# Channel attention and retention of a four-layer decoder rewritten as one pipeline of eight groups

## The chip, the core and the metric

The kernel runs on one core of one Trainium2 chip. The metric is the device time of one execution in microseconds (us), lower is better. Engines are named as the profile names them: PE (TensorE matmuls), PEld (TensorE weight loads), DVE (VectorE), ACT (ScalarE), POOL (GpSimd) and SP (SyncE, which here only issues DMAs and clears semaphores).

## The reference

A decoder of four layers on x of 8 sequences x 256 tokens x 128 channels, each layer a self part, a context part and a feed-forward part, each added to x behind a layer norm. The change touches the first two parts of layer 2; everything else stays. `x` is the activation, `ctx` the context (8 x 256 x 128), all in float32.

```python
# L2_attn (stage L2a): attention between channels, 8 heads of 16 channels
h = layernorm(x)
xn = h * rsqrt(mean(h * h) + 1e-6) * norm_weight
q, k, v = split(xn @ w_qkv.T)                       # each head: 16 channels x 256 tokens
q = l2norm(q over the tokens) * exp(temperature)
k = l2norm(k over the tokens)
attn = softmax(q @ k.T)                             # 16 x 16 per head, from a sum over the tokens
x = x + (attn @ v, heads joined) @ w_out.T

# L2_xattn (stage L2x): retention against the context
h = layernorm(x)
q = xpos(h @ Wq);  k = xpos(ctx @ Wk, inverse scale);  v = ctx @ Wv
scores = (q @ k.T) * mask                           # mask[i, j] = 0.96875 ** (i - j) for i >= j, else 0
x = x + scores @ v
```

`xpos` rotates neighbouring channels: a product with a cosine table plus a product of the swapped channels with a sine table.

## The kernel before

The program is a sequence of stages (`STAGES`: L0a, L0x, L0f, L1a, L1x, L1f, L2a, L2x, L2f, L3a, L3x, L3f). x stays in SBUF for the whole program as 16 token tiles of 128 x 128 (`core.X`), and the context lies there transposed (`core.ctxT`). Each stage is one block with a program for each engine, tied by semaphores. At a boundary every engine drains, SP waits for all four (`end_pass_sync`, L195), clears all semaphores of the stage one by one (`ALL_STAGES` plus the stage's list in `PASS_SEMS`) and lets the engines go on (L197).

The weights of a stage come in one DMA (`load_next_weights`, L174), issued at the start of the stage before, into one of two buffers `stage_W`. The 4 MB of expert weights of L2f are issued at the start of L2a (`load_ffn`, L1402).

`channel_attention` (L2a) first norms all 16 tiles at once: statistics (L219, L222), a root on ACT as exp(-0.5 ln) (L258, L259) with one Newton step on DVE (L236 to L239), apply (L243). It does the whole of this twice, for the layer norm and then for the RMS norm of its result, turns the 16 tiles on PE (L268) and copies them out (L1491). Then comes a boundary and a loop of four passes (`NPASS`), each for two sequences (four tiles), each with a boundary at its end. A pass: queries, keys and values channel-major (L1451), sums of squares on ACT (L1500), root and Newton step (L1506, L1507, L1532 to L1538), queries and keys scaled (L1541), turned to token-major (L1456) and copied (L274), the product over the tokens (L1462), mask, maximum, exponential, normalisation (L1545 to L1553), the result turned (L1467) and copied, times the values (L1472), copied, times the output weights (L1477), added to x (L281).

`retention` (L2x) computes all values from the context (L1592), norms all 16 tiles at once, turns them, and has four passes with a boundary each: keys and queries and their swapped forms (L1601), the rotation on DVE (L1649 to L1651), scores (L1607, L1609), decay (L1653, L1654), output (L1617, L1620), added to x (L281). POOL does nothing in either stage.

All PE operands of the two stages are float32, and a float32 matmul shows as two instructions in the trace, a transpose as one.

## Time and profile before

| what | value |
|---|---|
| three runs | 1805.43, 1817.75, 1818.41 us (median 1817.75) |
| the profiled execution | 1812.71 us, its span 1810.9 us |
| busy over the span | PE 1278.4, PEld 805.9, DVE 1026.2, ACT 604.7, POOL 556.3 us |
| mean granted clock of TensorE | 0.846 of full speed |
| L2a and L2x | from 1012.00 to 1203.24 us |

The span runs from the first to the last instruction. The chain that ended last, as the page shows it, lies in the last stage and says nothing on L2a and L2x, so these two are read from the timeline and the windows. The granted clock is 0.50 at 1.2 GHz and 1.00 at 2.4 GHz, and a mean between them is a stretch with both.

### The profile page before, as it was taken

The page shows a single profiled execution, that of the slowest core. Times are in us where ns is not written, and L with a number is a line of the kernel's source. Part 1 is how long each engine was busy: PE and PEld are TensorE (multiplying, and loading weights), DVE is VectorE, ACT ScalarE, POOL GpSimd, SP SyncE. Part 2 cuts the span into 40 slices and gives each one's busy share as a digit, 9 for nine tenths or more (in the row PEclk, how much of TensorE's full clock was granted, in tenths as well). Part 3 has the DMA queues.
Part 4 walks back from the last instruction along what each step waited for, and adds up shares of the span by engine and source line. Part 5 has one row for each costly group of instructions (what it writes and reads, how often), then busy time and mean ns, then how long its engine had stood idle before and what let it go on. Part 6 is the DMA issues. An engine that isn't in the chain of part 4 may idle for free. (4 is left out here: it accounts for less than half of the span.)

```text
span 1810.9 us, 30796 instructions
## 1 busy us (share of the span) xinstructions
PE 1278.4 (71%) x9105; PEld 805.9 (45%) x9105; DVE 1026.2 (57%) x4304; ACT 604.7 (33%) x1441; POOL 556.3 (31%) x931
## 2 busy tenths in 40 slices
PE   0289999995392799999739255645677765996686
PEld 0146555553291456555329133435644432553332
DVE  0478787764776777777267522456533346773432
ACT  0025554442040255556404112102232322664221
POOL 1256368873341544463034000004300003411000
PEclk9879999998596799999959655876878886998798
DMA  9633443300114334443011300001200004320000
GB/s 251 205 118 113 137 147 116 115 23 14 35 53 177 119 113 121 143 133 112 4 39 56 143 0 0 13 31 52 67 8 0 0 32 141 112 86 3 0 0 23
DMA packets 134311, 138.28 MB, mean 76 GB/s; under 512 B 11328, under 2 KB 106176, under 8 KB 133136
## 3 DMA queue, kind: packets, MB, share of 16 engines
q1 hardware_dynamic: 128208, 119.79, 21.5%
q0 software_dynamic: 5952, 16.68, 3.3%
q8 instruction: 70, 1.15, 0.3%
q14 instruction: 81, 0.66, 0.1%
HBM read 84.10 MB, written 49.70 MB: 74 GB/s over the span
## 5 line engine op out<-in xcount | busy, mean ns | idle before, releaser
L769 ACT ACTIVATE L0a_Pr<-PS 128x512 f32<-128x512 f32 (+1 forms) x256 | 137.1, 547 | 159.3 <-PE PS L678 94.2
L769 ACT ACTIVATE L1a_Pr<-PS 128x512 f32<-128x512 f32 (+1 forms) x256 | 136.2, 548 | 122.6 <-PE PS L675 65.0
L525 POOL TENSOR_TENSOR L0a_PG<-L0a_Pr,L0a_G 128x512 f32<-128x512 f32 x80 | 106.6, 1336 | 29.1 <-ACT L0a_Pr L769 17.1
L875 DVE CUSTOM_DVE_ANT_0 L1a_junk<-PS,L1a_neg 128x256 bf16<-128x256 f32 x256 | 94.7, 420 | 35.1 <-PE PS L653 34.9
L653 PE MATMUL PS<-L0a_Kst,L0a_Qm 128*128 128x256 bf16 (+1 forms) x512 | 94.7, 271 | 11.6 <-DVE L0a_mx L875 10.7
L653 PE MATMUL PS<-L1a_Kst,L1a_Qm 128*128 128x256 bf16 (+1 forms) x512 | 94.2, 270 | 11.6 <-DVE L1a_mx L875 10.6
L878 DVE TENSOR_REDUCE L3x_mx<-PS 128x2 f32<-128x512 f32 x128 | 83.7, 686 | 31.9 <-PE PS L653 31.5
L673 PE MATMUL PS<-L1a_Qm,L1a_Kst 128*128 128x512 bf16 (+1 forms) x256 | 91.0, 356 | 9.2 <-DMA L1a_Qm<-L1a_mT 6.0
L875 DVE CUSTOM_DVE_ANT_0 L1a_junk<-PS,causal_q 128x128 bf16<-128x128 f32 (+1 forms) x256 | 78.3, 352 | 30.2 <-PE PS L653 29.5
L875 DVE CUSTOM_DVE_ANT_0 L0a_junk<-PS,causal_q 128x128 bf16<-128x128 f32 (+1 forms) x256 | 78.3, 352 | 30.1 <-PE PS L653 29.4
L673 PE MATMUL PS<-L0a_Qm,L0a_Kst 128*128 128x512 bf16 (+1 forms) x256 | 90.8, 355 | 5.7 <-DMA L0a_Qm<-L0a_mT 2.9
L875 DVE CUSTOM_DVE_ANT_0 L0a_junk<-PS,L0a_neg 128x256 bf16<-128x256 f32 x192 | 72.8, 418 | 38.8 <-PE PS L653 38.2
L769 ACT ACTIVATE L3x_Pr<-PS 128x512 f32<-128x512 f32 x128 | 73.5, 603 | 46.2 <-PE PS L673 45.8
L675 PE MATMUL PS<-neg_k,ident_b 128*128 128x256 bf16 x256 | 70.1, 274 | 0.0
L653 PEld LDWEIGHTS PS<-L0a_Kst,L0a_Qm 128*128 128x128 bf16 x512 | 44.0, 102 | 57.0 <-DVE L0a_mx L875 32.4
L653 PEld LDWEIGHTS PS<-L1a_Kst,L1a_Qm 128*128 128x128 bf16 x512 | 43.7, 102 | 56.9 <-DVE L1a_mx L875 31.7
L1063 POOL MEMSET L2f_ends<- 128x4 f32 x2 | 0.1, 101 | 204.7 <-POOLq L1571 204.7
L703 PE MATMUL PS<-L1a_Pr,L1a_vaug 128*32 128x256 f32 (+1 forms) x1024 | 61.7, 358 | 0.2 <-ACT L1a_Pr L769 0.2
L653 PE MATMUL PS<-L3x_Kst,L3x_Qm 128*128 128x256 bf16 x256 | 51.9, 288 | 7.5 <-DVE L3x_mx L878 4.7
L673 PE MATMUL PS<-L3x_Qm,L3x_Kst 128*128 128x512 bf16 x128 | 48.8, 389 | 9.7 <-ACT L3x_Pr L769 5.1
L678 PE MATMUL PS<-L0a_neg,ident_b 128*128 128x512 bf16 x128 | 48.8, 381 | 0.0
L678 PE MATMUL PS<-L1a_neg,ident_b 128*128 128x512 bf16 x128 | 48.5, 379 | 0.0
(727 smaller groups left out, 3291.8 us busy)
## 6 DMA issues: line engine op xcount, KB each, us to landing
ffn_w_<-L_ffn SPq DMA_DIRECT2D x6, 2048.0 KB, 11.9
sorted_in<-zeros POOLq DMA_DIRECT2D x2, 4386.0 KB, 42.8
L0a_Kst<-k_image SPq DMA_DIRECT2D x64, 128.0 KB
L0a_Qm<-q_image SPq DMA_DIRECT2D x64, 128.0 KB
L1a_Kst<-k_image SPq DMA_DIRECT2D x64, 128.0 KB
L1a_Qm<-q_image SPq DMA_DIRECT2D x64, 128.0 KB
L3x_Kst<-k_image SPq DMA_DIRECT2D x32, 128.0 KB
L3x_Qm<-q_image SPq DMA_DIRECT2D x32, 128.0 KB
```

The lines of the kernel that those rows point to most:

```text
L525: g.tensor_tensor(PG[:, V_ % GATED_RING, :].rearrange("p (h q) -> p h q", h=2), Pr[:, V_ % RING, :].rearrange("p (h q) -> p h q", h=2), G[ ...
L653: ins = mm(PS[:, bank, par * nk:(par + 1) * nk], Qm[:, buf, par, hp, tt * P:(tt + 1) * P], Kst[:, buf, hp, 0:nk], start=(par == 0), stop=T ...
L673: ins = mm(o, Kst[:, buf, hp, kt * P:(kt + 1) * P], Qm[:, buf, :, hp, q0:S], start=True, stop=True, **free)
L675: ins = mm(o[:, :, 0:P], core.ident_b[:, :], core.neg_k[:, :].unsqueeze(1).broadcast_to([P, 2, P]), start=False, stop=True, **free)
L678: ins = mm(o, core.ident_b[:, :], neg[:, buf, 1, kt].unsqueeze(1).broadcast_to([P, 2, S]), start=False, stop=True, **free)
L703: ins = mm(o, vaug[:, buf, half, kt, 4 * g + j, :], src[:, par * nq:(par + 1) * nq], start=(kt == 0 and half == 0), stop=True, **free)
L769: a(Pr[:, V_ % RING, 0:2 * nq], PS[:, T_BANK + v % 2, 0:2 * nq], ACT.Exp, scale=SCALE)\
L875: ins = v.tensor_tensor_reduce(junk[:, tt, par, 0:nk], scored[:, par], off, 1.0, LOWEST, ALU.add, ALU.max, mx[:, i % 2, tt, par, hp:hp + 1])
L878: ins = v.tensor_reduce(mx[:, i % 2, tt, :, hp:hp + 1], scored, AX, ALU.max)
L1063: nc.gpsimd.memset(ends[k][:, 0:E // 2], 0.0).then_inc(s["pads"], 1)
```

## The change

`channel_attention` and `retention` are replaced by one function, `mixers`, without loops or boundaries inside. It works on eight groups of four tiles: four of channel attention, then four of retention. Every step of a group has a slot number (an offset plus four times the group's number; retention starts 25 slots later), each engine walks through the 55 slots (-8 to 46) in order and issues what falls into each, and semaphores alone tie the engines. Buffers are rings of two or three, a step waits until the step that last read its place is done, and `bank_empty` lets PE wait for the last reader of a PSUM bank from a table.

- The layer norm and the RMS norm of channel attention are merged: from the variance of the layer norm follows the mean square of its result, so there is one set of statistics and one apply, on ACT instead of DVE. The Newton steps run on POOL.
- Queries and keys come token-major from one matmul of 256 columns a tile, so that their transposes and copies go. They are squared on DVE, summed over the tokens by matmuls with one column of ones, and their product over the tokens is taken unscaled. The scales are applied to the 128x128 product, before and after it is turned.
- The output weights are multiplied with the normalised 128x128 matrix, and the values with the result, so that the output is token-major at once.
- Keys and values of retention are projected from the context between the channel groups; the rotated parts are added on POOL.
- SP issues the weights of L2f when the fourth channel output is done. Semaphores are taken per stage from now on (`core.open`), in all stages.

The core of the diff:

```diff
-SEMS = list(dict.fromkeys(KEEP + ALL_STAGES + sum(PASS_SEMS.values(), [])))
+SEMS = list(dict.fromkeys(KEEP + ALL_STAGES))
...
-def channel_attention(core):
+def mixers(core):
...
+    STATS, AGGR, VAR, ROOT, NEWTON, ROOT2, NEWTON2, APPLY, TURN, TURNED, PROJECT = -8, -7, -6, -5, -4, -3, -2, -1, 0, 1, 2
+
+    QK_OUT, SQUARE, V_OUT, GRAM, SUMS, SUM_ROOT, SUM_NEWTON, SCALE, TURN_G, MASK, EXP, SHARE, TIMES_WO, WO_OUT, TIMES_V, ADD = (
+        3, 4, 4, 5, 6, 6, 7, 8, 9, 10, 11, 12, 13, 14, 15, 16)
+
+    ROTATE_Q, JOIN_Q, SCORES, DECAY, OUT, ADD_B = 3, 4, 6, 7, 8, 9
+
+    KEYS = {0: -2, 1: 2, 2: 6, 3: 10}
+    VALUES = {0: (-2, G_BANK), 1: (1, TURN_BANK), 2: (5, TURN_BANK), 3: (12, V_BANK)}
+    base = lambda st, g: PER * g + (FIRST_B if st == "L2x" else 0)
...
+            def _(sp):
                 load_next_weights(core, sp)
                 load_ffn(core, sp, "L2")
+                sp.wait_ge(s["y_psum"], G)
+                core.at += 1
+                load_next_weights(core, sp)
...
+                def newton(out, start, of, r):
+
+                    step(g_.tensor_tensor(nsq[:, r], start[:, r], start[:, r], ALU.mult))
+                    step(g_.tensor_tensor(nsq[:, r], nsq[:, r], of[:, r], ALU.mult))
+                    step(g_.tensor_scalar(nsq[:, r], nsq[:, r], -0.5, 1.5, ALU.mult, ALU.add))
+                    step(g_.tensor_tensor(out[:, r], start[:, r], nsq[:, r], ALU.mult))
...
+                for n in SLOTS:
+                    for st, g, m in both(n, TURN):
+                        pe.wait_ge(s["xn_ready"], m + 1)
+                        bank_empty(n, XT_BANK)
+                        for t in range(T):
+                            ins = tr(PS[:, XT_BANK, t * P:(t + 1) * P], xn[:, m % R, t, :], w("ident"))
+                        ins.then_inc(s["xT_psum"], 1)
...
+                    g = group_at(n, "L2a", GRAM)
+                    if g is not None:
+                        r = g % R
+                        pe.wait_ge(s["sq_ready"], g + 1)
+                        bank_empty(n, G_BANK)
+                        for what in range(2):
+                            for t in range(T):
+                                at = 2 * P + what * NSEQ + t // TS
+                                mm(PS[:, G_BANK, at:at + 1], sq[:, r, t, what * P:(what + 1) * P], w("ones")[:, 0:1],
+                                   start=(what == 0 and t == 0), stop=(t % TS == TS - 1), **free)
+                        for t in range(T):
+                            b = t // TS
+                            ins = mm(PS[:, G_BANK, b * P:(b + 1) * P], qkT[:, r, t, P:2 * P], qkT[:, r, t, 0:P],
+                                     start=False, stop=(t % TS == TS - 1), **free)
+                        ins.then_inc(s["g_psum"], 1)
...
+                    g = key_group(n)
+                    if g is not None:
+                        if g == 0:
+                            pe.wait_ge(s["stage_w"], 16 * (core.at + 2))
+                        for k, name in enumerate(("L2x_k", "L2x_ks")):
+                            bank_empty(n, K_BANK + k)
+                            mm(PS[:, K_BANK + k, :], w(name), core.ctxT[:, g * NT:(g + 1) * NT], start=True, stop=True, **free)\
+                                .then_inc(s["k_psum"], 1)
...
+                    for st, g, m in both(n, APPLY):
+                        r = m % R
+                        act.wait_ge(s["ln_scale"], m + 1)
+                        if m >= R:
+                            act.wait_ge(s["xT_psum"], m - R + 1)
+                        for t in range(T):
+                            ins = a(xn[:, r, t, :], tile(g, t), ACT.Identity, scale=grow[:, r, t:t + 1], bias=shift[:, r, t:t + 1])
+                        ins.then_inc(s["xn_ready"], 1)
...
+                        v.tensor_tensor(sq[:, r], qkT[:, r], qkT[:, r], ALU.mult).then_inc(s["sq_ready"], 1)
...
+                            v.tensor_tensor(two(to[:, g % R, :]), two(PS[:, QK_BANK + k, :]), tab(name), ALU.mult).then_inc(s["q_turned"], 1)
```

Within a slot PE issues in this order: turns, small turn (TURN_G), output weights, values, Gram, channel projection, retention projection, keys, retention values, scores, output.

## Rows read from the trace of the kernel before

**Rows 1.** Windows: us, busy (instructions) of PE, PEld, DVE, ACT, POOL, granted clock, DMA.

```profile
1035.20:1059.80 24.60, 13.32 (x36) 8.22 (x36) 5.86 (x18) 5.67 (x18) 0.00 (x0) 0.57 0.00 0
...
1135.10:1147.70 12.60, 10.62 (x48) 8.66 (x48) 9.43 (x53) 4.88 (x10) 0.00 (x0) 0.76 0.14 44
...
1176.40:1189.30 12.90, 6.87 (x28) 4.13 (x28) 5.58 (x9) 0.00 (x0) 0.00 (x0) 1.00 0.00 0
...
1012.00:1205.00 193.00, 101.81 (x320) 64.64 (x320) 73.47 (x269) 31.30 (x90) 0.00 (x0) 0.67 0.08 30
```

**Rows 2.** Timeline where L2a starts: start us, us, engine, line, operation [idle before].

```profile
1004.90 4.02 DVE L1390 SCALAR_TENSOR_TENSOR X<-L1f_yg,L1f_gain,X 128x128 f32<-128x128 f32 x15
1011.96 0.35 SPq L174 DMA_DIRECT2D stage_W<-small_L2x  x1
1012.00 3.19 DVE L219 BATCH_NORM_STATS2 L2a_ln_st<-X 128x6 f32<-128x128 f32 x16 [3.09 <-PEq L1039]
```

**Rows 3.** Timeline of one channel attention pass and the boundary behind it.

```profile
1044.63 0.60 ACT L274 ACTIVATE L2a_qkt<-PS 128x512 f32<-128x512 f32 x1 [3.38 <-PE PS L1456]
...
1049.16 0.43 DVE L1548 TENSOR_TENSOR L2a_sm<-L2a_sm,L2a_rm 128x256 f32<-128x256 f32 x1
...
1057.37 0.69 DVE L281 TENSOR_TENSOR X<-PS,X 128x512 f32 x1 [6.22 <-PE PS L1477]
...
1060.17 2.07 PE L1451 MATMUL PS<-L2a_xT,stage_W 128*128 x2 [2.97 <-SPq L195]
```

**Rows 4.** Timeline of retention, from its values to the end of its last pass.

```profile
1135.36 6.59 PE L1592 MATMUL PS<-stage_W,ctxT 128*128 128x128 f32 x32 [3.16 <-PEq L1424]
...
1149.70 0.34 PEld L1601 LDWEIGHTS PS<-ctxT,stage_W 128*128 128x128 f32 x1 [0.52 <-issue]
1150.55 0.34 PEld L1601 LDWEIGHTS PS<-L2x_xT,stage_W 128*128 128x128 f32 x1 [0.52 <-issue]
...
1176.69 1.98 PE L1601 MATMUL PS<-ctxT,stage_W 128*128 x4 [2.46 <-SPq L195]
...
1185.49 0.71 PE L1617 MATMUL PS<-L2x_V,L2x_D 128*128 x4 [1.21 <-DVE L2x_D L1654]
...
1202.55 0.69 DVE L281 TENSOR_TENSOR X<-PS,X 128x512 f32 x1 [3.23 <-PE PS L1620]
1205.00 0.33 SPq L174 DMA_DIRECT2D stage_W<-small_L3a  x1
```

**Rows 5.** Timeline of L2f's first steps, and of L0f's activations.

```profile
1205.26 0.87 DVE L1210 BATCH_NORM_STATS2 L2f_st<-X 128x6 f32<-128x128 f32 x4
1206.16 0.38 DVE L1213 BATCH_NORM_AGGREGATE L2f_mv<-L2f_st 128x2 f32<-128x6 f32 x4
...
1212.74 1.72 PE L1095 MATMUL PS<-stage_W,L2f_xT 128*128 128x8 f32 x8
...
540.75 0.88 ACT L1195 ACTIVATE L0f_hT<-PS,stage_W 128x128 f32<-128x128 f32 x3 [1.01 <-PE PS L1145]
```

**Rows 6.** POOL's steps by tile and line: ns min/median/max; then two in time.

```profile
L489 POOL TENSOR_TENSOR L0a_nsq<-L0a_nsq,L0a_var x16: 194/196/582, 58.7 to 315.3; 128x2 f32<-128x2 f32 x16
L525 POOL TENSOR_TENSOR L0a_PG<-L0a_Pr,L0a_G x80: 1255/1272/1739, 248.4 to 427.4; 128x512 f32<-128x512 f32 x80
563.37 0.20 POOL L489 TENSOR_TENSOR L1a_nsq<-L1a_nsq,L1a_var 128x2 f32<-128x2 f32 x1
563.65 0.19 POOL L490 TENSOR_SCALAR L1a_nsq<-L1a_nsq 128x2 f32<-128x2 f32 x1
```

**Rows 7.** DMA issues in the two stages: KB each, median us to landing.

```profile
stage_W<-small_L2x SPq DMA_DIRECT2D x1, 960.0 KB, 4.7
```

**Rows 8.** Window at the start of retention: us, PE busy, granted clock, DMA.

```profile
1138.00:1141.00 3.00, 3.00 (x16) 0.50 0.09 36
```

**Rows 9.** ACT table loads: the one at the start, the next ones.

```profile
0.74 1.28 ACT L2136 ACT_TABLE_LOAD   x1 [0.74 <-PEq L2324]
L1806 ACT ACT_TABLE_LOAD  x4: 1283/1283/1283, 1330.8 to 1445.5; - x4
```

More of the change, by code:

```diff
@@ L157, in __init__, with open @@
         self.PS = ctx.enter_context(nc.psum_tensor("PS", [P, 8, 512], F32))
+    def open(self, stack, kind):
+        for n in PASS_SEMS[kind]:
+            self.sem[n] = stack.enter_context(self.nc.semaphore(n))
     def buffers(self, stack):
@@ L336, in attention @@
     with ExitStack() as c:
+        core.open(c, "attention")
         sb = core.buffers(c)
@@ L1409, in channel_attention @@
     with ExitStack() as c:
+        core.open(c, "mixers")
         sb = core.buffers(c)
[L1411 to L1419 removed]
@@ new lines, in mixers, with group_at, key_group @@
+        D0, D1 = sb("D0", [P, R, NSEQ, S]), sb("D1", [P, R, NSEQ, P])
+        tile = lambda g, t: core.X[:, g * T + t, :]
+        two = lambda ap: ap.rearrange("p (b t) -> p b t", b=NSEQ)
+        tab = lambda n: w(n).unsqueeze(1).broadcast_to([P, NSEQ, S])
+        def group_at(n, st, off):
+            g, r = divmod(n - off - base(st, 0), PER)
+            return g if r == 0 and 0 <= g < G else None
+        def key_group(n, late=0):
+            return next((g for g in range(G) if KEYS[g] + late == n), None)
@@ L1424, in channel_attention, with value_group, both @@
+        def value_group(n, late=0):
+            return next((g for g in range(G) if VALUES[g][0] + late == n), None)
+        def both(n, off):
+            for st in ("L2a", "L2x"):
+                g = group_at(n, st, off)
+                if g is not None:
+                    yield st, g, norm_of(st, g)
         with nc.Block() as block:
@@ L2172, in program @@
                 attention(core, (st,))
-            elif st in ATTN:
+            elif st == "L2a":
+                mixers(core)
+            elif st in ATTN or st == "L2x":
                 continue
@@ L2177, in program @@
             else:
-                {"L2a": channel_attention, "L2x": retention, "L3a": state_space, "L3f": latent_experts}[st](core)
+                {"L3a": state_space, "L3f": latent_experts}[st](core)
         finish(core)
```

536 lines of the change are left out of this document (327 added, 209 removed).

## The prediction

> **What bounds the kernel now.** Only the stages L2a and L2x are rewritten, so I first cut their stretch out. The timeline has the last work of the stage before them ending at 1004.90 + 4.02 = 1008.92 us and VectorE's first L2a instruction at 1012.00 [rows 2]; the last residual add of L2x ends at 1202.55 + 0.69 = 1203.24 and the next stage's weights are issued at 1205.00 [rows 4]. So the two stages take 191.2 us of work plus 1.8 us of boundary. The windows show in which way: over 193 us PE is busy 101.8, DVE 73.5, ACT 31.3 and POOL not at all, and these sum to 206.6 [rows 1]. Almost nothing runs beside anything else: a chain, not an engine, is the bound. The timeline of one pass says the same: each engine starts when the one before it ends, and from the add's end at 1058.06 to PE's next matmul at 1060.17 another 2.1 us go to the boundary [rows 3]. PE runs at a granted clock of 0.57 in a channel attention pass, 0.76 in the norm stretch of retention and 1.00 in one of its passes [rows 1]: of its two levels (1.2 and 2.4 GHz) it holds the low one most of the time in the first.
>
> **What is removed.** The stretch to 1035.20 (16 tiles normed at once, twice, on DVE, with PE idle), four passes of about 25 us, the norm stretch of retention to 1147.70, four passes of 12.9 us or more [rows 1] and nine of ten boundaries, of about 2 us each. What goes is the whole 191.2 us; I therefore build the new stage from zero.
>
> **The new work per engine.** A float32 matmul is two instructions. Where PE is fed, one instruction of 512 columns takes 0.85 us at the low clock (its weight loads follow at 1149.70 and 1150.55) and 0.43 at the high one (four take 1.98 with their tail) [rows 4]. Of 128 columns 32 instructions take 6.59 us at the low clock, 0.206 each, and at the high clock four take 0.71 with their tail, 0.11 each [rows 4]. PE per channel group at the low clock: 4 turns 0.85, queries and keys (8 instructions of 256 columns) 3.4, values 1.7, the Gram product 1.7, two small turns 0.43, times the output weights 0.85, times values 1.7. The sums of squares are 16 instructions with one moving column and a full weight load each; eight with 8 columns span 1.72 us [rows 5], so I take 0.213 each, 3.4. Together 14.1 us low, 7.0 high. A retention group: turns 0.85, queries 3.4, keys 3.4, values 1.7, scores 2.6, output 2.6: 14.5 low, 7.3 high. Four of each: 114 us low, 57 high. The old kernel has about as much, so PE's work is not what is saved.
>
> DVE per pair of groups: two norms' statistics at 0.87 + 0.42 [rows 5] + 0.2 for a small step each; squares of 128x1024, not shown, for which I extend 0.43 at 256 and 0.69 at 512 elements to 1.22 [rows 3, 4]; scale 0.62, mask and maximum 1.3, share 1.15, rotations 2.5, decay 1.1, two adds 1.4, two small 0.4. About 12.7, times four 51 us. ACT: copies of 512 columns at 0.60 [rows 3], roots 0.45, four applies 1.1 a norm (three of that shape take 0.88 [rows 5]): 8.5 a pair, 34 us. POOL gets 25 small instructions a pair, 0.27 us from one start to the next, and two adds of 128x512, for which the nearest row is a product at 1.27 [rows 6]: 6.8 + 2.6 = 9.4, times four 37 us. No engine comes near 191 us. PE is first, and the rest is a question of the chain.
>
> **The new chain, in five stretches, from 1012.00 = 0.** (1) Start. The norm of group 0 is DVE 1.5, roots 0.45, POOL 6 steps 1.65, roots 0.45, POOL 7 steps 1.95, apply 1.1: 7.3 us. But keys and values of group 0 stand ahead of the first turn on PE's queue, and they wait for the L2x weights, which land 4.7 us after issue [rows 7]; 3.4 + 1.7 at the low clock end at 9.8. The turn waits for them, so the start is 9.8 us. (2) Turn (0.45 to 1), copy 0.7, projection 1.7, ACT's copies behind the apply of group 1, squares 1.2: 6.7 more until the first Gram product. Then PE is fed: per group 0.4 turn, 2.6 projection, 2.6 Gram and sums, 1.7 keys, 0.85 values, and small ones: 8.2 us at the high clock. Everything else of a group between two PE steps (sums 0.2, roots 0.45, POOL 1.65, scale 0.6: 2.9 us) is covered by the next group's projection and keys (4.3 us). Three such periods make 24.6, and the first residual add stands at 41.1. (3) From there no new channel group enters. Group 3 still has Gram 2.4, sums and roots 0.7, POOL 1.65, scale 0.6, turn 0.3, mask 1.35, exponential 0.6, share 1.2, output weights 0.7, copy 0.45, times values 1.1: 11.1, and 1.9 of queueing on DVE behind group 2 and the first retention norms: 13, to 54. The retention norms run in here and cost nothing, but PE's queue puts the projection of retention group 0 behind the times-values of channel group 3, so the two halves scarcely overlap. (4) Retention runs in a loop through PE and DVE: scores 1.4, decay 1.15, output 1.5, next projection 1.8, i.e. 5.9 us a group; keys and values are done by then. First projections and the wait for the joined queries (DVE 1.35, POOL 1.3) to 60, then two loops and the last group's scores, decay, output and add to 79. (5) To this comes what the ideal leaves out: in stretch 3 PE has only 4 to 5 us of work in 13 and I expect it back at the low clock, where it stays until retention has run some us, as it did when PE had worked from 1135.36 on without a break and still had 0.50 until 1141 [rows 8]. That is 5 us. POOL beside a busy DVE: 3 us. In-order queues whose head waits for a late one: 3 us. Sum 90 us.
>
> Bounds of what no row shows: the small POOL steps are 0.195 at the median and 0.582 at most [rows 6]; 25 of them lie on the path (13 at the start, 6 for group 3, 6 for the last retention group), so the gain is none and the loss at most 25 x 0.39 = 9.7 us; I take 3, as the median is near the low end. The clock: all high from the start takes off 5 to 11 us, all low is the third case below. An instruction with one column could cost less than one with 8, but its weight load stands either way; if the load were hidden better, at most 1.5 us of each period's 1.7 go, 4.5 in three periods. ACT gets Identity with scale and bias in place of DVE's subtraction; an ACT table load is 1.28 us [rows 9], and if each of the 8 norms paid two it would be 20.5 us. The first stage uses Identity (line 759) between exponentials, and from 0.74 to 1330.8 us there is no load at all [rows 9], so I take nothing.
>
> The Trainium skill has a rule against this change. The trace shows an identical small POOL step between 0.194 and 0.582 us, and the 128x512 product up to 1.739 [rows 6]. "GPSIMD Engine Reference" (section 1, Specifications) says that POOL's SBUF interfaces are shared with VectorE and contend with instructions that read two SBUF inputs. By it the squares, a product of two SBUF operands, would hold the Newton steps up and the upper bound above would be the likelier end. The bound itself, 25 steps at 0.582, puts 6.7 us more into the sum: 96.7 us, 1720. I give it 0.15 of the chance, inside the forecast's.
>
> **Edits at nothing.** The weights of L2f are now issued when the fourth channel output is done (about 54), and nothing stands behind them on SP's queue but the end of the stage at 90. Without that cover they would cost what the L2x weights take to land, 4.7 us [rows 7], at most. The expert weights keep their place. Semaphores opened per stage issue nothing in between. The closing boundary clears 44 semaphores instead of 17; one with 43 took 1011.96 - 1008.92 = 3.0 us [rows 2] and the one with 17 took 1.8, so 1.3 us come on top.
>
> **The sum.** The profiled execution took 1812.71 us, a span of 1810.9 and 1.8 around it; it is 0.3% under the median 1817.75 and inside the runs shown (1805.43 to 1818.41). 1812.7 - 191.2 + 90 + 1.3 = 1713 us.
>
> **The rivals.** *Ideal pipeline:* high clock throughout, no queueing; the stage takes 75 to 81 us, 1698 to 1704. For it: PE is 80% busy in both fed stretches. Against it: stretch 3. *Clock stays low:* in a channel pass PE was busy 13.3 of 24.6 us and held 0.57 [rows 1]; if the new bursts look like that to the chip, nothing speeds PE up. ("TensorE: Matmul & The Clock Gate" of the Trainium skill, Part 1, has it so: "the default state is throttled, and activity releases the throttle".) At that level the start keeps its 9.8 us, stretch 2 is 8 + 3 x 16.4 = 57, stretch 3 is 16 with its 3 us of PE doubled, and retention has a loop of 2.6 + 1.15 + 2.8 + 3.5 = 10 us: 12 for the first projections, two loops, 9 for the last group, 41. Sum 124 us, 1747. Partly low gives 1725 to 1747. Against it: at the low clock PE would be busy nine tenths of stretch 2, more than in the passes that held 1.00 with 6.87 of 12.90 us [rows 1]. *No overlap at all:* the waits added on the rings (each step on the step two groups back, each bank on its last reader) tie the in-order queues so that one engine works at a time. Then the stage is the sum of the busy times at the low clock, 114 + 51 + 34 + 37 = 236 us, 1859: slower. It decides once less than 46 us of these 236 is hidden (236 + 1.3 - 191.2). The slot order, where a group's next step is at least one slot later and another group's work stands between, speaks against it. *The halves don't merge:* that part of the change I already count as not doing what its name says; were it to, stretch 3 would shrink by 8 us, 1705.
>
> **How the numbers follow.** Forecast, 1705 to 1725: 0.58. Ideal or merging, below 1705: 0.18. Partly or wholly low clock, 1725 to 1750: 0.19. ACT table loads or another stall of 20 us or more on top: 0.03. No overlap: 0.02. The range leaves out the last two, the upper end of the low clock and little below 1695: 1695 to 1738. A measurement of this kernel can tell about 1% from no change, and the forecast is 5.8% under the median: faster 0.96, same 0.02, slower 0.02.
>
> **What would show it.** The stage from its first statistics to the last add 82 to 102 us; first turn at 9.8 and waiting for keys, not for the norm; PE at 1.00 in stretch 2 with 8.2 us a group; a gap-ridden stretch of about 13 us with a low clock before the first retention projection; retention at 6 us a group; POOL steps at 0.2; one boundary of 3 us. Wrong would be: PE idle in stretch 2 with DVE or POOL named as releaser, ACT table loads, POOL steps at half a us, or later stages changed by more than 2 us.

## The result, and the profile of the changed kernel

| | before | after |
|---|---|---|
| median (runs) | 1818.08 us (4) | 1723.18 us (4) |
| lowest to highest | 1805.43 to 1819.68 | 1720.67 to 1726.39 |
| after over before, 95% interval | | 0.9508 [0.9472, 0.9545] |
| profiled execution, its span | 1812.71, 1810.9 us | 1726.39, 1724.6 us |
| busy PE, DVE, ACT, POOL | 1278, 1026, 605, 556 us | 1262, 1001, 609, 590 us |
| L2a and L2x together | 1012.00 to 1203.24 | 1016.89 to 1114.66 |

The change makes the kernel 4.9% faster. Busy time hardly moves; the two stages go from 191.2 us to 97.8 us. The windows of the changed kernel cut them at the marks of my prediction. The first row runs to the first sums of squares, the next three from one group's sums to the next group's, the fifth (stretch 3) to the first projection of retention, the sixth to the last residual add. The columns are those of [rows 1].

```profile
1016.90:1035.20 18.30, 10.60 (x42) 6.69 (x42) 9.29 (x38) 9.27 (x28) 10.62 (x38) 0.78 0.70 284
1035.20:1049.50 14.30, 11.98 (x52) 9.82 (x52) 4.39 (x11) 5.27 (x15) 6.27 (x22) 0.78 0.00 1
1049.50:1062.00 12.50, 11.37 (x56) 8.77 (x56) 5.35 (x14) 5.32 (x13) 3.83 (x14) 0.86 0.01 2
1062.00:1070.90 8.90, 7.35 (x48) 6.24 (x48) 4.61 (x14) 2.94 (x8) 1.30 (x6) 1.00 0.00 0
1070.90:1089.30 18.40, 14.04 (x62) 12.17 (x63) 10.16 (x48) 7.24 (x24) 4.73 (x23) 0.54 0.00 0
1089.30:1114.70 25.40, 20.37 (x110) 14.79 (x109) 14.40 (x30) 5.44 (x14) 6.49 (x12) 1.00 0.07 22
sum 97.80, PE 75.71 PEld 58.48 DVE 48.21 ACT 35.48 POOL 33.24; mean PE 12.62 PEld 9.75 DVE 8.03 ACT 5.91 POOL 5.54
```

The busy times now sum to 193 us in 98 (without the weight loads), where before 207 stood in 193 [rows 1]. The granted clock is the second thing to see: 0.78 and 0.86 in the first two of the three periods from one group's sums to the next, where I expected 1.00, and 0.54 in stretch 3.

PE's timeline at the start shows what the first turn waits for, and then the place where the first surprise sits.

```profile
1021.57 3.37 PE L1645 MATMUL PS<-ctxT,stage_W 128*128 128x512 f32 x4 [18.45 <-DMA stage_W<-small_L2x]
...
1025.67 0.60 PE L1580 MATMUL PS<-W,L2a_xn 128*128 128x128 f32 x4
...
1035.21 1.01 PE L1613 MATMUL PS<-W,L2a_sq 128*128 128x1 f32 x4 [2.77 <-DVE L2a_sq L1834]
```

DVE and POOL in those microseconds, from the timeline of all engines, and the same pair one group later:

```profile
1032.04 0.69 DVE L1841 TENSOR_TENSOR L2a_ks<-PS,stage_W 128x512 f32<-128x512 f32 x1 [0.17 <-PE PS L1645]
1032.65 0.86 DVE L1771 BATCH_NORM_STATS2 L2a_st<-X 128x6 f32<-128x128 f32 x4
1032.81 1.26 POOL L1555 TENSOR_TENSOR L2a_rk<-L2a_kc,L2a_ks 128x512 f32<-128x512 f32 x1 [2.05 <-DVE L2a_ks L1841]
1033.43 1.73 DVE L1834 TENSOR_TENSOR L2a_sq<-L2a_qkT 128x1024 f32<-128x1024 f32 x1
1034.04 1.18 POOL L1509 TENSOR_TENSOR L2a_nsq<-L2a_r 128x4 f32<-128x4 f32 x1
...
1047.48 2.00 DVE L1834 TENSOR_TENSOR L2a_sq<-L2a_qkT 128x1024 f32<-128x1024 f32 x1
...
1048.36 1.18 POOL L1509 TENSOR_TENSOR L2a_nsq<-L2a_r 128x4 f32<-128x4 f32 x1
```

ACT had the queries and keys of group 0 copied out at 1031.53, but the squares start at 1033.43: a rotation product of the retention keys and the statistics of a later norm stand ahead of them on DVE's queue. Then they take 1.73 us, and 2.00 the next time, where I had 1.22. The rows show how: POOL's add ends at 1034.07 and 1048.39, and both times the squares end 1.09 us behind it, nearly their whole 1.21 us; and POOL's next step, 1.18 us instead of 0.20, ends within 0.1 us of the squares. In both places the two engines take turns rather than slow each other a little. The view of the tile L2a_sq gives all four squares, and what waited for them:

```profile
L1834 DVE TENSOR_TENSOR L2a_sq<-L2a_qkT x4: 1212/1472/1996, 1033.4 to 1069.7; 128x1024 f32<-128x1024 f32 x4
...
  DVE L2a_sq L1834: 12.2, 8
```

One square takes 1.21 us, as extended from [rows 3, 4], the slowest 2.00. The 12.2 us are waits of PE and of its weight loads, which the view counts apart (6.5 for the loads, 5.7 for PE itself).

In stretch 3, PE's timeline has gaps, the longest of them 1.87 us, and DVE's says why group 3 comes so late:

```profile
1078.49 0.69 PE L1587 MATMUL PS<-W,L2a_gs 128*128 128x128 f32 x2
...
1079.00 0.52 DVE L1820 TENSOR_SCALAR L2a_en<-L2a_ex,L2a_rd 128x128 f32<-128x128 f32 x2
1079.40 0.68 DVE L1827 TENSOR_TENSOR X<-PS,X 128x512 f32<-128x512 f32 x1
1080.12 0.87 DVE L1771 BATCH_NORM_STATS2 L2a_st<-X 128x6 f32<-128x128 f32 x4
...
1081.32 0.58 DVE L1806 SCALAR_TENSOR_TENSOR L2a_sm<-PS,L2a_rs,stage_W 128x128 f32<-128x128 f32 x2
...
1083.52 1.63 ACT L1704 ACTIVATE L2a_xn<-X,L2a_shift,L2a_grow 128x128 f32<-128x128 f32 x4
...
1085.21 1.12 PE L1580 MATMUL PS<-W,L2a_xn 128*128 128x128 f32 x4 [1.87 <-ACT L2a_xn L1704]
1086.12 1.06 PE L1594 MATMUL PS<-stage_W,L2a_en 128*128 128x128 f32 x4
1087.65 1.91 PE L1602 MATMUL PS<-L2a_mo,L2a_vT 128*128 128x128 f32 x8 [0.47 <-ACT L2a_mo L1739]
1089.40 1.88 PE L1638 MATMUL PS<-L2a_xT,stage_W 128*128 128x512 f32 x4
```

The product of group 3 is turned (L1587) at 1079.18, and its mask (L1806) starts 2.1 us later, behind group 2's share and add and the norm of a retention group. Its matrix is ready for the output weights (L1594) at 1084.45, and PE doesn't start that product until 1086.12, since the turn of retention group 0 (L1580) stands ahead and waits for ACT's apply. At the end of the stage the last add and the next stage's first DMA stand 3.57 us apart:

```profile
1113.97 0.69 DVE L1827 TENSOR_TENSOR X<-PS,X 128x512 f32<-128x512 f32 x1 [1.70 <-PE PS L1677]
1118.23 0.33 SPq L179 DMA_DIRECT2D stage_W<-small_L3a  x1
```

### The profile page after: what moved, and what is told of

It reads as the page before. It is cut to its first block and busy times, and to the rows that moved or that the text cites. A ratio compares the mean times of both kernels' runs of the same rounds, so it can differ in the third digit from the quotient of the medians.

```text
span 1724.6 us, 30567 instructions
## 1 busy us (share of the span) xinstructions
PE 1262.1 (73%) x9153; PEld 805.3 (47%) x9153; DVE 1001.0 (58%) x4187; ACT 609.2 (35%) x1452; POOL 589.8 (34%) x1043
## 3 DMA queue, kind: packets, MB, share of 16 engines
q8 instruction: 72, 1.18, 0.3%
## 5 line engine op out<-in xcount | busy, mean ns | idle before, releaser
L659 PE MATMUL PS<-L0a_Kst,L0a_Qm 128*128 128x256 bf16 (+1 forms) x512 | 95.8, 274 | 11.2 <-DVE L0a_mx L881 10.4
L881 DVE CUSTOM_DVE_ANT_0 L1a_junk<-PS,causal_q 128x128 bf16<-128x128 f32 (+1 forms) x256 | 78.3, 352 | 30.3 <-PE PS L659 29.6
L775 ACT ACTIVATE L3x_Pr<-PS 128x512 f32<-128x512 f32 x128 | 73.5, 603 | 42.3 <-PE PS L679 42.1
L659 PEld LDWEIGHTS PS<-L0a_Kst,L0a_Qm 128*128 128x128 bf16 x512 | 44.7, 103 | 57.0 <-DVE L0a_mx L881 31.6
L585 PE MATMUL PS<-W,L0a_xn 128*128 128x128 f32 x32 | 8.6, 360 | 55.4 <-POOL L0a_xn L501 55.4
## 6 DMA issues: line engine op xcount, KB each, us to landing
ffn_w_<-L_ffn SPq DMA_DIRECT2D x6, 2048.0 KB, 11.7
```

Source lines behind the costliest of these rows:

```text
L659: ins = mm(PS[:, bank, par * nk:(par + 1) * nk], Qm[:, buf, par, hp, tt * P:(tt + 1) * P], Kst[:, buf, hp, 0:nk], start=(par == 0), stop=T ...
L775: a(Pr[:, V_ % RING, 0:2 * nq], PS[:, T_BANK + v % 2, 0:2 * nq], ACT.Exp, scale=SCALE)\
L881: ins = v.tensor_tensor_reduce(junk[:, tt, par, 0:nk], scored[:, par], off, 1.0, LOWEST, ALU.add, ALU.max, mx[:, i % 2, tt, par, hp:hp + 1])
```

## The experiments

Twelve runs of eleven kernels (the later turn was run twice). Those with one run beside the kernel before are compared by the length of the stage in the profile, which the two executions of the later turn gave to 0.1 us (85.6 and 85.7), while whole times of one kernel differ by several us. That is one pair; the column up to the first sums shows that parts of the stage can move by a us without an edit there. Each row of the table is cut at the same marks (us):

| kernel | to first sums | three periods | fourth sums to retention | retention | stage |
|---|---|---|---|---|---|
| predicted | 16.5 | 24.6 | 13 | 25 | 79.1, with 11 on top 90 |
| after | 18.3 | 35.7 (14.3, 12.5, 8.9) | 18.5 | 25.3 | 97.8 |
| squares on ACT | 16.9 | 32.0 (9.7, 13.4, 8.8) | 16.8 | 25.3 | 90.9 |
| wide ones | 19.1 | 34.3 (13.0, 12.4, 8.9) | 17.2 | 25.3 | 95.9 |
| keys later | 17.2 | 29.4 (8.6, 10.9, 9.9) | 18.0 | 25.7 | 90.3 |
| ACT and wide | 17.4 | 27.6 (9.7, 10.2, 7.7) | 17.1 | 26.5 | 88.6 |
| ACT, wide, keys | 17.5 | 27.0 (9.0, 10.2, 7.7) | 17.1 | 25.3 | 86.9 |
| the same, filled | 17.4 | 27.5 | 17.5 | 25.3 | 87.6 |
| later turn | 17.4 | 27.0 | 15.3 | 25.9 | 85.6 |
| later turn, norms last | 17.1 | 26.9 | 16.5 | 27.0 | 87.6 |
| later turn, filled | 17.4 | 27.5 | 14.9 | 25.3 | 85.0 |

**1. Is it the overlap or the shorter work?** The same instructions, with the slots so far apart that no two groups overlap.

```diff
-    PER, R = 4, 2
+    PER, R = 26, 2
-    FIRST_B = 25
+    FIRST_B = 103
```

> The same steps, but each group starts 26 slots after the one before it and retention behind all of channel attention (103 slots), so that no two groups overlap; keys and values of the context keep their slots. If the gain is the overlap, as the prediction's chain has it, the stage from the first statistics to the last add is the sum of the chains: about 33 us for a channel group at the low clock and 18 for a retention group, 190 to 210 us, as long as the old kernel's 191 in spite of nine boundaries less. If the shorter work (merged norms, no transposed copies, no boundaries) brought a good part by itself, the stage would be 140 to 165 us.

One run: 1828.26 us, against 1812.75 of the kernel before beside it. The stage takes 202.7 us, inside the 190 to 210 expected if the gain is the overlap; channel groups stand 30.3 to 31.6 us apart and retention groups 18.0 to 19.6. The old kernel had 191.2, that is about 30 us a channel group with its share of the norms and 17 a retention group. Two lines of PE's timeline in one group show the old picture of engines that take turns:

```profile
1071.57 0.69 PE L1587 MATMUL PS<-W,L2a_gs 128*128 128x128 f32 x2 [3.20 <-DVE L2a_gs L1797]
1075.51 1.22 PE L1594 MATMUL PS<-stage_W,L2a_en 128*128 128x128 f32 x4 [3.26 <-DVE L2a_en L1820]
```

The window over this stage (1014.70 to 1217.40 us) shows why the shorter work brings nothing by itself. DVE's work did shrink, from 73.5 us [rows 1] to 48.5, but ACT has 7.5 us more and POOL 32.4 where it had none, so that the sum over the four engines rises from 206.6 to 220.8 us. PE's 101.1 us are the old 101.8, at nearly the old clock (0.64 for 0.67). Without overlap nothing of the gain is left. With overlap the same PE work takes 75.7 us, since PE is granted more of its clock. How much the merged norms and the missing transposes add once there is overlap is not shown.

**2. The squares.** They become one Square activation per group on ACT:

```diff
-                        v.tensor_tensor(sq[:, r], qkT[:, r], qkT[:, r], ALU.mult).then_inc(s["sq_ready"], 1)
+                        a(sq[:, g % R].rearrange("p t c -> p (t c)"), qkT[:, g % R].rearrange("p t c -> p (t c)"), ACT.Square)\
+                            .then_inc(s["sq_ready"], 1)
...
```

> The squares (128x1024) move from VectorE to ScalarE, as one Square activation of about 1.15 us right behind the copy of queries and keys. Theory A: PE waits for the squares (2.8 and 1.5 us before the first two Gram products), because they stand behind key rotations and statistics on VectorE's queue and are drawn out to 1.73 and 2.00 us beside POOL's additions; then the waits shrink to under 1 us, POOL's step of 1.18 us beside them returns to 0.20, and the stage falls from 97.8 to about 91. Theory B (PE's clock falls behind the one-column matmuls whatever PE waits for): the waits shrink, but the clock still falls in the same three places and the stage falls by 2 to 3 us at most.

One run: 1717.49 us, stage 90.9. The wait for squares is gone and the first period falls from 14.3 to 9.7 us. The stage comes out as the first of the two theories has it (91), but the clock falls all the same, as in the second. The second period stays long: behind a wait of 0.87 us PE is busy without a gap from 1044.16 on, and the clock falls.

```profile
1034.70:1044.40 9.70, 8.82 (x52) 6.90 (x53) 3.56 (x15) 7.45 (x20) 6.05 (x22) 1.00 0.00 0
1044.40:1047.50 3.10, 3.10 (x22) 3.10 (x21) 0.00 (x0) 0.09 (x1) 1.91 (x8) 0.70 0.01 3
1047.50:1052.00 4.50, 4.50 (x15) 3.78 (x15) 1.27 (x5) 3.01 (x9) 1.30 (x6) 0.50 0.02 4
```

```profile
1044.16 0.44 PE L1587 MATMUL PS<-W,L2a_gs 128*128 128x128 f32 x2 [0.87 <-DVE L2a_gs L1804]
1044.43 2.31 PE L1613 MATMUL PS<-W,L2a_sq 128*128 128x1 f32 x16
```

From 1044.43 PE runs the sums of squares, 16 instructions with one moving column each in 2.31 us, and the projection after them runs at 0.50. In this kernel's third period (0.81) the clock falls behind the same sums once more, in its first (1.00) it doesn't.

**3. Is it the one moving column?** The sums are taken with all 128 columns of the ones, so that PE's instructions carry columns; their result goes to the bank of the values.

```diff
-                                mm(PS[:, G_BANK, at:at + 1], sq[:, r, t, what * P:(what + 1) * P], w("ones")[:, 0:1],
...
+                                mm(PS[:, V_BANK, at:at + P], sq[:, r, t, what * P:(what + 1) * P], w("ones"),
...
```

> The sums of squares move 128 columns of ones in place of one, into a bank of their own; the weight loads stay and set the pace in both, so the 16 instructions take the same time at the same clock. Theory B: the clock falls because PE moves next to no columns for 1.9 us or more in each group; then the granted clock stays near 1.00 through the fed stretch, the sums take 1.9 us in all groups and the stage falls from 97.8 to about 88. Theory A: the clock falls in the waits for the squares; then the clock has the same pattern and the stage stays within 2 us of 97.8.

One run: 1714.06 us, stage 95.9. Alone it gives 1.9 us, within the 2 us that the theory of the waits allows and far from the 88 of the other: the clock still falls where PE has waited for squares, and not in the third period. 1.3 of the 1.9 us lie in stretch 3, whose sums now run at the high clock. The windows, with the wait in the first row:

```profile
1030.00:1032.00 2.00, 0.01 (x1) 0.01 (x1) 2.00 (x5) 0.00 (x0) 1.99 (x2) 1.00 0.00 0
1032.00:1036.00 4.00, 4.00 (x21) 4.00 (x22) 0.40 (x5) 0.00 (x0) 1.22 (x6) 0.57 0.00 0
```

At the high clock the wide instruction costs hardly more than the narrow one: 16 of them span 2.02 us (kernels of experiment 5) against 1.95.

**4. Out of each other's way.** The rotation products of the retention keys, which stand ahead of the squares on DVE and whose sum runs on POOL beside them, come one slot later.

```diff
-    KEYS = {0: -2, 1: 2, 2: 6, 3: 10}
+    KEYS = {0: -2, 1: 3, 2: 7, 3: 11}
```

> The key projections of groups 1 to 3 move one slot later (3, 7, 11 in place of 2, 6, 10), so their rotations stand behind the squares on VectorE, not in front of them, and POOL's addition follows later too. Theory A: the wait before the first Gram product falls from 2.8 us to about 1, the squares are back at 1.22 us, and the stage falls by 3 to 6 us. Theory B: at most 2 us.

One run: 1714.82 us, stage 90.3. The tiles of this kernel:

```profile
L1834 DVE TENSOR_TENSOR L2a_sq<-L2a_qkT x4: 1216/1222/1226, 1034.8 to 1064.2; 128x1024 f32<-128x1024 f32 x4
...
  DVE L2a_sq L1834: 3.1, 4
...
L1509 POOL TENSOR_TENSOR L2a_nsq<-L2a_r x12: 195/198/202, 1020.9 to 1088.5; 128x4 f32<-128x4 f32 x12
```

All squares take 1.22 us, none of the twelve first steps of a Newton iteration is above 0.202, and the wait falls from 12.2 to 3.1 us. Moving three numbers in a table gives 7.5 us, more than the 3 to 6 expected. Not all of it is the queue: of the 6.3 us in the three periods, PE's busy time gives 3.6 (30.7 to 27.1), since the first two periods now have a clock of 1.00, with the one-column sums in place, and 2.7 are shorter gaps. In the third (0.83) the clock falls behind those sums. The slow squares and the slow POOL step come and go together with their being side by side.

**5. Both causes of the clock at once.** Squares on ACT and wide ones; then the later keys too.

> Squares on ScalarE and 128 columns of ones, both at once. With the squares on ScalarE alone PE was hardly idle and its clock fell all the same behind the sums of the second group; with the wide ones alone it fell where PE waited. If each has its own part (theory C: the clock falls where the array moves few columns, be it in a wait or in one-column matmuls), then with both the granted clock stays at 1.00 from the first group to the fourth Gram product and the stage (first statistics to the last add) is 91.0 less 4 to 6 us, about 86. If one of them alone does it, the stage stays at 91.

One run: 1699.38 us, stage 88.6, where I expected 86. The whole is lower than any other execution of this family, but the stage begins at 1007.18, some 4 us before that of the next kernel, so the stage is what I go by. The clock holds through all four groups and falls only in stretch 3:

```profile
1019.00:1058.00 39.00, 34.45 (x206) 27.14 (x206) 15.40 (x57) 23.65 (x60) 15.87 (x62) 1.00 0.05 21
1058.00:1070.00 12.00, 8.50 (x31) 6.87 (x32) 7.76 (x34) 5.73 (x17) 3.40 (x17) 0.50 0.01 2
```

> The same with the key projections one slot later. Theory C: they no longer matter, since nothing on VectorE's queue stands before the squares any more: within 1.5 us of the run without them. If the order of VectorE's queue delays other steps too (the scales of the product, the maximum), another 2 to 3 us go.

Median 1708.84 us of 4 runs, ratio to before 0.9468 [0.9422, 0.9514]; stage 86.9, 1.7 less than without the later keys. Only 0.6 of that lies in the periods, so the keys hardly matter there any more; 1.2 lie in retention, which began at a low clock in the one execution (0.74 over its first 4.7 us) and not in the other. The three periods now take 27.0 us with 25.4 of PE work at a clock of 1.00, so a fed PE needs 8.5 us a group and 0.5 us go in gaps: 9.0, not my 8.2. In all seven executions with squares on ACT and wide ones (experiments 5, 6, 8 and 9) the clock is 1.00 in all three periods. No wait of PE in them is longer than 0.9 us. Some of these waits, up to 0.7 us, are for the copy of the values (L1761), whose bank the wide sums use too. What is shown is that this pair of edits holds the clock. That one-column sums alone bring it down is not: they stood in the first period of the kernel with squares on ACT, in two periods of the one with later keys and in the third of the changed kernel, all at 1.00. Every fall in these periods came shortly behind a wait of 0.7 us or more, but not every such wait was followed by one.

```profile
1028.50:1055.50 27.00, 25.42 (x157) 20.53 (x157) 10.64 (x31) 17.11 (x41) 11.61 (x42) 1.00 0.01 1
```

**6. Is stretch 3 long because of its low clock?** The kernel of the row above, with three float32 matmuls of 128 columns (of the identity and ones, result unused) ahead of PE's waits in the slots 17 to 27.

```diff
+                def fill(n):
+                    if 17 <= n <= 27:
+                        bank = XT_BANK if n < 25 else V_BANK
+                        bank_empty(n, bank)
+                        for t in range(3):
+                            mm(PS[:, bank, t * P:(t + 1) * P], w("ident"), w("ones"), start=(t == 0), stop=True, **free)
...
+                        fill(n)
                         pe.wait_ge(s["xn_ready"], m + 1)
...
```

> On top of that, from slot 17 to slot 27 PE issues three extra float32 matmuls of 128 columns (0.65 us at the high clock, their result unused) ahead of each wait for the small turns, the output weights, the values and the first retention turns: nine times, 5.8 us. If stretch 3 is long because its clock is low, the clock stays at 1.00, the stretch from the fourth Gram product to the first retention projection falls from 18 to 14 or 15 us and the stage by 3 us. If it is long because the chain through VectorE, ScalarE and POOL is, the filler stands in the way and the stage gets 1 to 4 us longer.

Median 1708.68 us of 4 runs, ratio 0.9459 [0.9414, 0.9504]; stage 87.6, 0.7 longer, so that neither of the two expectations is met. The filler holds the clock for 12 us of the stretch; behind the wait of 2.62 us for ACT's apply it is lost again (0.68 in the rest). The stretch is as long as before:

```profile
1058.45:1070.60 12.15, 9.44 (x78) 8.70 (x76) 7.92 (x38) 4.03 (x15) 3.18 (x15) 1.00 0.01 2
1070.60:1075.97 5.37, 4.75 (x28) 4.75 (x29) 1.89 (x10) 2.60 (x9) 1.12 (x6) 0.68 0.00 0
```

17.5 us against 17.1. In the order of that kernel the filler gives nothing back. That doesn't make the low clock free: the filler's own work stands partly on the path (group 3's output weights start 1.2 us later than without it), and experiment 9 separates the two somewhat. How a low clock lengthens this stretch shows where it is low from the start. In the changed kernel group 3's sums and Gram product end with the clamp of the sums (L1788) 4.4 us behind their start; in the kernel with ACT, wide and keys, at 1.00, it is 2.9. Nearly all of these 1.5 us arrive at the end: the two stretches take 18.5 and 17.1.

**7. The merged norm alone, in the old kernel.** The kernel before, with one set of statistics and one apply in L2a.

```diff
...
-                dve_layernorm(core, dve, step, L, lambda t: L["xn"][:, t, :], f2, s["xh_ready"], n=1,
-                              rms=True, eps=1e-6, tiles=ALL_TILES)
...
+                        step(v.tensor_tensor(L["w"][:, 1], L["r"][:, 0], L["r"][:, 0], ALU.mult))
+                        step(v.tensor_tensor(L["w"][:, 1], L["w"][:, 1], mv[:, :, 1], ALU.mult))
+                        v.tensor_scalar(L["w"][:, 1], L["w"][:, 1], 1e-6, None, ALU.add).then_inc(s["ln_mv"], 1)
...
```

> The kernel before, with one part of the change alone: channel attention's two norms merged (one set of statistics, one apply, the second root from the first variance), all on VectorE over 16 tiles as before. The second statistics (3.2 + 1.2 us) and the second apply (the slower of the two stays, 4.2 us, the other 3.2 goes) fall away, five small steps of 0.2 come on: the stage falls from 191.2 to about 183.5 us.

One run: 1809.7 us against a median of 1802.62 of the kernel before beside it. L2a gets 7.3 us shorter (113.7 against 121.05), as expected. But L2x, in which not a line differs, takes 78.4 us against 67.9, so the two together don't fall to 183.5 and get 3 us longer. The windows of 56 us up to its end, before (all four passes) and with the merged norm (the last three and a half of them):

```profile
1147.70:1203.30 55.60, 32.99 (x112) 20.13 (x112) 22.34 (x36) 0.00 (x0) 0.00 (x0) 0.88 0.00 0
```

```profile
1147.00:1203.00 56.00, 36.27 (x96) 22.76 (x96) 17.84 (x29) 0.00 (x0) 0.00 (x0) 0.65 0.00 0
```

Passes of the same code are granted 0.88 of the clock in one kernel and 0.65 in the other. Over the whole of L2x PE's busy time goes from 43.6 to 53.9 us for the same 160 instructions, which is nearly all of the 10.5 us. This is one execution each, so that the shift does it is not shown; that a lower clock can take back the gain is.

**8. Is stretch 3 long because of the order of the queues?** On top of the kernel with ACT, wide and keys, retention comes one slot later, so that its first turn stands behind the output weights of channel group 3 on PE's queue.

```diff
-    FIRST_B = 25
+    FIRST_B = 26
```

> All retention steps come one slot later, so that the first retention turn stands behind the product with the output weights of channel group 3 on PE's queue, not ahead of it. Theory (stretch 3 is long because of the order of the queues, not because of the clock): that product no longer waits for ACT's apply, and the time from the fourth group's sums to the first retention projection falls from 17.1 us to about 15; the stage falls from 86.9 to about 85 us. Rival (another queue head takes over, for instance the mask behind the norm of retention group 1 on DVE, or the later turn delays the projection by as much): within 1 us of 86.9.

One run: 1706.14 us, stage 85.6, the stretch 15.3 us (17.1 without it), as the theory of the queues had it. The timeline of PE, where the turn no longer waits:

```profile
1063.52 1.23 PE L1594 MATMUL PS<-stage_W,L2a_en 128*128 128x128 f32 x4 [0.78 <-DVE L2a_en L1828]
1064.54 1.06 PE L1580 MATMUL PS<-W,L2a_xn 128*128 128x128 f32 x4
1065.39 1.92 PE L1602 MATMUL PS<-L2a_mo,L2a_vT 128*128 128x128 f32 x8
1067.10 2.53 PE L1639 MATMUL PS<-L2a_xT,stage_W 128*128 128x512 f32 x4
```

Then DVE's statistics, aggregates and variances are moved behind mask, share, add, rotation and decay within each slot:

> On top of the later turn, DVE's statistics of the layer norms are issued last within each slot, behind mask, share, add, rotation and decay. Theory (queue order): the mask of channel group 3 starts within 0.5 us of its turned product instead of 2 us behind it, and the stretch from the fourth sums to the first retention projection falls to 13 or 14 us; the stage takes 83 to 84 us and the whole about 1705. Rival (queue order is not what counts, or the late statistics delay the applies by as much): no change within 1 us against the run with the later turn alone, 1707 to 1709.

A miss. The median of 6 runs is 1704.85 us, ratio 0.9426 [0.9387, 0.9465], which is no different from the others; but the stage of the profiled execution takes 87.6 us, 2.0 more than with the later turn alone. The mask comes earlier, 1.1 us behind its turned product instead of 1.9 (0.5 was expected), and the output weights of group 3 start 11.2 us behind the fourth sums instead of 11.7. The turn of retention group 0 then waits for the late norm, with the last times-values of channel attention behind it, and the low clock lasts into the projection (3.61 us against 2.53):

```profile
1060.04 1.22 PE L1594 MATMUL PS<-stage_W,L2a_en 128*128 128x128 f32 x4 [0.29 <-DVE L2a_en L1810]
1062.73 1.12 PE L1580 MATMUL PS<-W,L2a_xn 128*128 128x128 f32 x4 [1.47 <-ACT L2a_xn L1705]
1063.64 1.92 PE L1602 MATMUL PS<-L2a_mo,L2a_vT 128*128 128x128 f32 x8
1065.35 3.61 PE L1639 MATMUL PS<-L2a_xT,stage_W 128*128 128x512 f32 x4
```

**9. With the queues in order, does the clock count?** The later turn with the filler, and the later turn once more, timed in turns on one chip.

> The later retention turn together with the filler matmuls (three float32 matmuls of 128 columns ahead of PE's waits in the slots of stretch 3), which keep PE at 1.00 there. With the old order they gained nothing, since the chain waited in the queues. If the clock counts once the queues are in order, PE's own work of the stretch runs at the high clock: the times-values of group 3 falls from 1.92 to about 1.05 us, the projection behind it from 2.53 to 1.9, the product with the output weights from 1.23 to 0.71, and the two of group 2 likewise; the fourth sums to the first retention projection go from 15.3 to 13 us, the stage from 85.6 to 83 us. Rival (the filler's own 0.9 us at each wait lies on the path and eats that): 85 to 87 us.

> The kernel with the later retention turn once more, timed in rounds beside the filled one. The stage again 85 to 86 us, the whole 1704 to 1710; the difference to the filled kernel is then read on the same chip. Theory (the clock counts with the queues in order): 2 us above the filled one. Rival: the same within 1 us or below it.

Filled: 1705.51 us (1703.93 to 1714.65, 5 runs), ratio 0.9435 [0.9410, 0.9460]; stage 85.0, stretch 14.9 us at a clock of 1.00 throughout. Not filled: 1707.15 (1705.64 to 1708.83, 5 runs), ratio 0.9432 [0.9416, 0.9449]; stage 85.7, stretch 15.3 us. PE's last three products did get as short as I expected (times-values 1.06 us, output weights 0.71), but up to its output weights the chain of group 3 runs over DVE, ACT and POOL, and takes 11.7 us from the fourth sums with the filler and without. Behind them the filler stands on the path, twice 0.67 us from one start to the next. The rival is right on what the filler brings: 0.6 us of stage, and nothing that shows in the whole time. The clock itself is worth more than that. An estimate from these rows: 0.6, plus 0.5 that the filler costs in the third period (8.2 for 7.7), plus about 1.1 of the 1.3 us between output weights and projection (ACT's copy ends at 1067.31 and the times-values start at 1068.50), together some 2 us.

The three timed kernels with the later turn, all built on squares on ACT, wide ones and later keys, take 0.943 of before, where the change itself takes 0.951. Their intervals overlap, so that no order among them is shown. All three lie below the interval of the change, [0.9472, 0.9545], if narrowly: the 10 to 13 us of stage appear in the whole time as 0.8%.

## Why the prediction was right, step by step

Forecast 1713, measured median 1723.18, inside the range. The profiled execution is 13.6 us above the sum, which was 1712.8 before rounding. That divides into 7.8 us of stage (97.8 for 90), 0.5 us of boundary, and 5.4 us in stages that the change doesn't touch: the stage begins at 1016.89 and not at 1012.00, and what follows it takes 606.4 us instead of 605.9. The 4.9 us ahead of the stage are of the size by which executions of one kernel differ, as in the later turn, whose stage began at 1007.4 in one and 1011.7 in the other.

That the number fits so well is partly luck. The four stretches took 18.7 us more than their 79.1: 1.8 up to the first sums, 11.1 in the periods, 5.5 in stretch 3 and 0.3 in retention. The 11 us of lumps cover most of it, but 5 of them were put down for a low clock in stretch 3 and at the start of retention, and most of the excess came in the stretch that I had called fed. Of the signs that I had named for being wrong one did appear: PE idle in stretch 2 with DVE as releaser, 2.77 and 1.48 us ahead of the sums of the first two groups. "PE at 1.00 in stretch 2 with 8.2 us a group" failed too. Sizes of work came out well: DVE 48.2 us for 51, ACT 35.5 for 34, POOL 33.2 for 37.

**Step: a chain bounds the stages, and work of the same size overlaps.** Right, and shown: without overlap the new code is no faster (experiment 1). PE's busy time of 75.7 us is between my 57 at the high clock and 114 at the low one.

**(1) Start 9.8 us, the turn waits for keys.** Right in kind, 8.8 us measured: the keys at 1021.57 wait for the weights, 4.7 us after their issue at 1016.84. From the first turn to the first sums it then took 9.5 us for my 6.7; PE's wait of 2.77 us for the squares is the difference.

**(2) Three periods of 8.2 us.** This is the term that was mis-sized: 14.3, 12.5 and 8.9, together 35.7 for 24.6. Three causes. The squares came late and slow, because I costed their duration without looking at what stands ahead of them on DVE, and took POOL's interference only for POOL's own steps: moving the keys by a slot gives back 6.3 us of the periods, 2.7 of them in gaps and 3.6 by a higher clock. The clock fell in what I had called fed: behind waits, and in some places behind the one-column sums, which I had costed in time alone; squares on ACT, wide ones and later keys together bring the periods to 27.0. Of the last 2.4 us, 0.8 are PE work that I had too small (25.4 for 24.6; my 8.2 leaves 0.05 us for the small turns, output weights and times-values) and 1.6 its gaps.

**(3) 13 us of stretch 3, and 5 + 3 + 3 on top.** The chain took 18.5. That the halves don't merge was right. That the low clock is part of the price holds, at less than my 5 us: its sums and Gram product took 1.5 us longer than at 1.00, and for the rest an estimate of some 2 us in a later order (experiment 9) is all that the runs give. The 3 us that I had put down for in-order queues are the right name, and the 1.9 us of queueing on DVE the right place: PE's turn waiting for ACT's apply costs 1.8 us (experiment 8). The mask starts 2.1 us behind its turned product, but letting it start earlier gave only 0.5 (experiment 8). An apply of four tiles takes 1.63 and not 1.1 us; I had scaled it from three activations of another kind.

**(4) Retention 25 us.** 25.3, with 5.74 us from one group to the next (predicted 5.9). The clock is 1.00 from its first projection on, so nothing of the 5 us of low clock falls here.

**(5) The lumps.** With the 79.1 they came within 7.8 us of 97.8; the 5 for the low clock belonged in good part to the periods. POOL's steps: median 0.198 us, and in 12 first steps of a Newton iteration (L1509) two of 1.18. The rule of the Trainium skill that I had weighed ("GPSIMD Engine Reference", section 1) is borne out where the squares, a product of two SBUF operands, run beside POOL. It didn't work in the way in which I had priced it, each step somewhat slower up to 0.58; it hit few steps hard, and VectorE's instruction as well. By that way its 6.7 us would have brought me nearer, for the wrong reason.

**The rivals.** The ideal pipeline fails in stretches 2 and 3. *Clock stays low* came true in part: 0.78 and 0.86 in the first two periods, 0.54 in stretch 3. I had argued against it that PE would be busy nine tenths of the stretch; it was busy 11.98 of 14.30 and 11.37 of 12.50, and lost the clock in part all the same. "TensorE: Matmul & The Clock Gate" of the Trainium skill (Part 1) has activity release the throttle; this agrees with 0.54 in stretch 3, where PE had 14.04 busy of 18.40 us. The sentence alone doesn't explain experiment 2, where the clock fell while PE had been busy without a gap since its last wait. What decides it there is open. *No overlap* is what experiment 1 builds, at 202.7 us rather than the 236 of the bare sum: the busy times there sum to 220.8 us, PE's part being 101 and not 114, and the rest overlaps even there. No table load of ACT appears in the stage.

**Edits at nothing.** The boundary with 44 semaphores took 3.57 us, 1.8 more than with 17 (predicted 1.3). The L2f weights were issued at 1089.59, 28.6 us ahead of the next stage, and no instruction there waited for them.

## What to carry to other kernels

When stages are rewritten as one pipeline, the gain is the overlap; price it by the busiest engine. Then read each in-order queue at the place where an urgent instruction stands behind one that isn't, since there the ideal is lost: 7.5 us came back from moving one group of instructions by a slot, 1.3 from moving another. An engine's busy time says nothing on whether its clock holds: behind a wait of PE, and in some places behind weight loads for one moving column each, what came next ran at half speed. Judge such edits by the length of the stage in the profile, since the whole time of one kernel scatters by more than they give.

## What the runs showed of the hardware

- The granted clock fell to 0.50 with PE busy without a gap since a wait of 0.87 us, while and after it ran 16 float32 instructions of one moving column (windows of the kernel with squares on ACT). In seven executions in which these carried 128 columns and no wait ahead was longer than 0.9 us it stayed at 1.00. With one column it also stayed at 1.00 in four places, so that more than the columns decides. The wide ones cost 0.07 us more in 16.
- Two-input work of DVE and POOL on SBUF beside each other: the squares 1.22 us alone, 1.73 and 2.00 beside POOL's add; a POOL step of 128x4 elements 0.20 alone and 1.18 beside the squares. POOL's add, which had started first, didn't get longer (1.26); the squares ended 1.09 us behind it both times, and the POOL step with them. In these two places the later one waited for the earlier.
- The same retention code had 0.88 of the clock in one kernel and 0.65 in another whose earlier stage was 7 us shorter, and L2x took 10.5 us more (one execution each).
